# A windowed-attention kernel on one core: the order of transfers, transposes and maxima inside a slot, 32x32 masks and three-operand normalisations

## The chip, the cores and the metric

The kernel runs as one program on 1 core of one Trainium2 chip. The metric is device time in microseconds (us) from one execution, taken as the median of several runs; lower is better.

## The reference

Two layers over x of 8 batches x 1024 rows x 256 features, each with a residual: windowed attention with 16 heads of 16 features, and a linear layer with the signs of a weight.

```python
def _L0_attn_ref(x, Wq, bq, Wk, bk, Wv, bv, Wo, bo):
    ...
    q = (x @ Wq.T + bq).reshape(B, S, N_HEADS, D_K)
    k = (x @ Wk.T + bk).reshape(B, S, N_HEADS, D_K)
    v = (x @ Wv.T + bv).reshape(B, S, N_HEADS, D_K)
    scores = jnp.einsum('bqhd,bkhd->bhqk', q, k) * SCALE
    scores = jnp.where(mask, scores, jnp.float32(-10000.0))   # key j with i - 128 <= j <= i
    attn = jax.nn.softmax(scores, axis=-1) + jnp.float32(1e-09)
    ctx = jnp.einsum('bhqk,bkhd->bqhd', attn, v).reshape(B, S, D_MODEL)
    return ctx @ Wo.T + bo
x = x + _L0_attn_ref(_layernorm(x), ...)
x = x + jnp.einsum('bsi,oi->bso', _layernorm(x), jnp.sign(weight))
```

## The kernel before

The rows are cut in tiles of 128, eight to a batch (t = 0 to 7), 64 in all, and two neighbouring tiles make a pair. All engines run the same loop of 64 **slots**, one for each tile, and four more for what is left over; the function slot of each engine is an order written out by hand, and semaphores alone connect the engines. In slot t the engines work on many tiles at once (function parts): the scores and the exponentials of tile t, the row maxima of tile t+3 (mx) and their transpose for tile t+2 (nm), probabilities times values of tile t-1 (pv), the output projection of tile t-3 (op), the second layer of tile t-4 (ff), and the load of the residual rows for tile t-2 (xr). Work on pairs alternates: slots with odd t project queries and values of pair (t+5)/2 (tqv) and load x; slots with even t project keys of pair (t+4)/2 (k) and compute the statistics and the first layer normalisation (ln). Below, an odd slot and an even one are meant in this sense, and the two together are called a slot pair.

**TensorE** computes, in a slot: scores in eight steps (two heads each, into two banks sc), the transposes of the unnormalised sums u (turn_u, into bank ga), the transpose of the maxima (turn_max), three groups of masked maximum scores (max_scores, bank mx), three groups of pv, and the projections. turn_u writes ga, so it waits until VectorE has read the output projection of the tile before it out of ga (semaphore x2_done). In max_scores a matmul of the 128x128 identity with a window of zeros and -1e30 first writes the mask of 2 or 3 heads for one of two row groups; 32x32 tiles with 16 rows of contraction then add the scores, 8 at a time side by side.

**VectorE**, in the order of a slot: second normalisation (norm2, tile xn2, shown as xn<-x), reciprocal and product of the sums (normalise), row_max 0, split parts of the projections (_lo tiles), k_lo in an even slot, row_max 1, statistics (ln), the residual sums x, q_lo in an odd slot, row_max 2, first normalisation norm1 in an even slot (xn<-xs), then the sum x2 = ga + xr, which releases turn_u of the next slot, and its statistics (mv) for norm2 of the next slot.

**GpSimd (POOL)**: two affine selects on 128x1024 values (mask_probs) for the second half of the heads of tile t-1, sum_v in an even slot, add_biases (adds brow to xr, which must have landed), rsqrt1 in an even slot (rs1 for norm1), mask_probs for the first half of tile t, and rsqrt2 (rs2 for norm2).

**SyncE (SP)** issues nearly all DMAs, in order; a wait holds back everything behind it. The queries in three parts are copied from the layout of the projection to q_stack by six DMAs for a pair (stack_q), behind two for q_max; the keys likewise (stack_k, set_k_max). stack_q stands in the odd slot in which the queries are projected, and waits for q_16, the last of ScalarE's copies of them. The lines after it in that slot are the load of xr and the store of y:

```python
                if part["tqv"]:
                    stack_q(*part["tqv"])
                if part["k"]:
                    set_k_max(*part["k"])
                if part["ks"]:
                    stack_k(*part["ks"])
                if part["xr"]:
                    load_xr(*part["xr"])
```

Of the kernel before, what the change touches and what calls it, by code (L numbers as in the profile page):

```python
# [23 lines left out]
P = 128  # L24
# [22 lines left out]
def build(nc, x, wq_t, wk_t, wv_t, wo_t, wf_t, bq_c, bk_c, bv_c, bo_r, out):  # L47
# [7 lines left out]
    with ExitStack() as ctx:  # L55
# [22 lines left out]
        window = sb("window", [P, 3, WIN], BF16)  # L78
        window0 = sb("window0", [P, 3, WIN], BF16)
# [122 lines left out]
        def parts(b, t):  # L202
# [34 lines left out]
        def _(sp):  # L237
# [6 lines left out]
            def stack_q(b, p):  # L244
                i, _ = halves(p)
                cols = slice(2 * P * p, 2 * P * (p + 1))
# [4 lines left out]
                for c in range(C):  # L251
                    sp.dma_start(q_max[64 * c:64 * c + DK, :, 2 * P * (g % 2):2 * P * (g % 2 + 1)],
                                 q_16[:, c, :]).then_inc(q_max_set[i], 16)
                wait(sp, sc_filled, SC_FILLS * (TILES * (b - 1) + 2 * p + 2))
# [4 lines left out]
                for c in range(C):  # L259
                    for r, src in enumerate((q_hi, q_hi, q_lo)):  # L260
                        at = 64 * c + DK * r
                        sp.dma_start(q_stack[at:at + DK, :, cols].bitcast(F32),  # L262
                                     src[:, c, :].bitcast(F32)).then_inc(q_stacked[i], 16)
# [27 lines left out]
            def stack_nmax(b, t):  # L291
                i, _ = halves(t)
                sp.wait_ge(nm_done, TILES * b + t + 1)
                for c in range(C):
# [10 lines left out]
            def slot(b, t):  # L305
                now, part = parts(b, t)
                if part["nm"]:
                    stack_nmax(*part["nm"])
                if part["load"]:
                    load_x(*part["load"])  # L310
                if part["tqv"]:
                    stack_q(*part["tqv"])
                if part["k"]:
                    set_k_max(*part["k"])
                if part["ks"]:
                    stack_k(*part["ks"])
                if part["xr"]:
                    load_xr(*part["xr"])
# [9 lines left out]
            stack_q(0, 0)  # L328
# [8 lines left out]
            stack_q(0, 1)  # L337
# [4 lines left out]
            stack_q(0, 2)  # L342
# [5 lines left out]
        def _(pool):  # L348
# [8 lines left out]
            g.memset(window[:, 0, :], 0.0)  # L357
            g.memset(window0[:, 0, :], 0.0).then_inc(pool_setup, 1)
# [4 lines left out]
            def make_windows():  # L363


                n = 3
                for mask in (window, window0):
                    for blk in range(P // QB):
                        m = mask[QB * blk:QB * (blk + 1), 0, :]
                        for base, cm, step in ((0, -1, 1), (P, 1, -1)):  # L370
                            pool.wait_ge(pool_setup, n)
                            g.affine_select(out=m, in_=m, compare_op=ALU.is_ge, fill=MASKED, base=base,
                                            pattern=[[step, WIN]], channel_multiplier=cm).then_inc(pool_setup, 1)
                            n += 1
                for blk in range(P // QB):
                    m = window0[QB * blk:QB * (blk + 1), 0, :]
                    pool.wait_ge(pool_setup, n)
                    g.affine_select(out=m, in_=m, compare_op=ALU.is_ge, fill=MASKED, base=QB * blk - P,
                                    pattern=[[1, WIN]], channel_multiplier=0).then_inc(pool_setup, 1)
                    n += 1  # L380
                pool.wait_ge(pool_setup, n)

                for mask in (window, window0):
                    for h in (1, 2):
                        last = g.tensor_copy(mask[:, h, :], mask[:, 0, :])
                last.then_inc(windows_done, 1)
# [74 lines left out]
        def _(act):  # L461
# [79 lines left out]
            def nmax_part(b, t):  # L541
# [4 lines left out]
                wait(act, nmax_stacked[i], 32 * (TILES // 2 * b + m))  # L546
# [76 lines left out]
        def _(dve):  # L623
# [20 lines left out]
            def norm1(b, p):  # L644
# [6 lines left out]
                for j in range(2):  # L651
                    last = v.tensor_scalar(xn[:, j], xs[:, i, j], mv1[:, j, 0:1], rs1[:, j:j + 1],  # L652
                                           ALU.subtract, ALU.mult)
                last.then_inc(xn_done, 1)

            def norm2(b, t):
# [5 lines left out]
                v.tensor_scalar(xn2[:, :], x2[:, i], mv2[:, 0:1], rs2[:, :],  # L662
                                ALU.subtract, ALU.mult).then_inc(xn2_done, 1)
# [66 lines left out]
            def slot(b, t):  # L730
                now, part = parts(b, t)
                if part["ff"]:
                    norm2(*part["ff"])
                if part["op"]:
                    normalise(*part["op"])
                if part["mx"]:
                    row_max(*part["mx"], 0)
# [93 lines left out]
        def _(pe):  # L831
# [72 lines left out]
            def max_scores(b, t, i, turns=(mx_banks,)):  # L904
# [10 lines left out]
                hs = slice(0, len(heads))  # L915
                for rg in range(C):
                    dst = banks[:, rg, 0:WIN * len(heads)].rearrange("p (h e k) -> p h e k", h=len(heads), k=QB)
                    if t == 0:
# [283 lines left out]
```

## Time and profile before

| | |
|---|---|
| median of 3 runs | 953.24 us (949.41, 953.24 and 1605.7) |
| profiled execution | 948.12 us, of which the traced span is 946.4 us |
| TensorE busy | 788.6 us, 83% |
| VectorE busy | 630.9 us, 67% |
| ScalarE busy | 487.9 us, 52% |
| GpSimd busy | 443.9 us, 47% |
| mean granted TensorE clock | 0.887 |

The chain of waits starts at the last instruction and goes back to what released each. A share of it belongs to work that nothing hid. The timeline shows instructions in order, merged where equal ones follow each other; the bracket at a row's end is the idle time of that engine ahead of it and what ended it.

### The profile page before, as it was taken

To read this page: it belongs to the slowest core of one execution; us is meant where nothing else is said; L and a number is where in the kernel's file an instruction comes from. 1 tells how busy PE (TensorE), PEld (TensorE's weight loads), DVE (VectorE), ACT (ScalarE), POOL (GpSimd) and SP (SyncE) were. 2 spreads that over 40 slices of the span, in tenths; PEclk is the share of its full clock that TensorE was granted. 3 is DMA by queue.
4 is the path that set the end of the run, shared out by engine and by line. 5 is a ranking of instruction groups with operands and counts; after the bars stand their busy time and mean duration, and the time that the engine had idled before them with its cause. 6 is when DMAs were issued, how large, how long until landed. Compare 5 with 4: busy or idle time off the path is not lost.

```text
span 946.4 us, 29257 instructions
## 1 busy us (share of the span) xinstructions
PE 788.6 (83%) x11920; PEld 643.7 (68%) x11920; DVE 630.9 (67%) x1171; ACT 487.9 (52%) x1029; POOL 443.9 (47%) x596
## 2 busy tenths in 40 slices
PE   2679898888888988888988888899888899888984
PEld 2467677776677766777776766777666777766763
DVE  6555667676767766776667766667667677666543
ACT  2245665555556554555645555565545565454640
POOL 6324444545535453544445454354444444545551
PEclk9767999889889997989979998988988999887995
DMA  3884656556646555775556677555567645457310
GB/s 94 113 105 84 106 93 97 94 83 114 113 79 106 90 94 88 114 113 85 89 86 102 95 114 109 93 95 83 86 106 113 102 86 87 92 79 108 65 34 22
DMA packets 105077, 87.80 MB, mean 93 GB/s; under 512 B 12336, under 2 KB 104944, under 8 KB 104944
## 3 DMA queue, kind: packets, MB, share of 16 engines
q1 hardware_dynamic: 103008, 84.49, 55.8%
q8 instruction: 95, 1.56, 0.8%
q10 hardware_dynamic: 1936, 1.45, 0.5%
q14 instruction: 38, 0.31, 0.1%
HBM read 18.22 MB, written 8.39 MB: 28 GB/s over the span
## 4 chain that ended last, share of the span: by engine, by line
PE 49%; DMA 15%; SPq 12%; DVE 10%; issue 6%; POOL 6%; ACT 1%; POOLq 0%; DVEq 0%; ACTq 0%
DMA xr<-x 14%; SPq L262 12%; PE sc L965 10%; PE gc L838 10%; PE pv L983 8%; PE ga L838 6%; PE mx L931 4%; DVE xn L652 4%; PE ga L994 2%; POOL rs L394 2%; POOL xr L428 2%; PE gc L853 2%; PE mx L923 2%; PE gb L1023 1%; DVE x L779 1%
## 5 line engine op out<-in xcount | busy, mean ns | idle before, releaser
L537 ACT ACTIVATE prob<-sc 128x512 f32<-128x512 f32 x448 | 264.3, 596 | 216.5 <-PE sc L965 212.6
L965 PE MATMUL sc<-q_stack,k_stack 128*128 128x256 f32 (+1 forms) x1024 | 249.9, 334 | 5.2 <-DMA q_stack<-q_hi 2.5
L965 PEld LDWEIGHTS sc<-q_stack,k_stack 128*128 128x128 f32 x1024 | 171.7, 210 | 53.7 <-issue 45.7
L695 DVE TENSOR_REDUCE nmax<-mx 128x6 f32<-128x960 f32 x188 | 195.1, 1038 | 10.0 <-PE mx L931 5.6
L983 PE MATMUL pv<-prob,v_ones 128*32 128x128 f32 x3840 | 159.0, 297 | 0.0
L420 POOL TENSOR_SCALAR_AFFINE_SELECT prob<-prob 128x1024 f32<-128x1024 f32 x128 | 143.9, 1124 | 5.9 <-ACT prob L539 5.9
L428 POOL TENSOR_TENSOR xr<-xr,brow 128x256 f32<-128x256 f32 x64 | 46.7, 730 | 189.6 <-DMA xr<-x 172.7
L417 POOL TENSOR_SCALAR_AFFINE_SELECT prob<-prob 128x1024 f32<-128x1024 f32 x112 | 122.3, 1092 | 25.1 <-ACT prob L537 25.1
L994 PE MATMUL ga<-ident,u 128*128 128x128 f32 x256 | 45.6, 307 | 89.8 <-DVE x L779 89.6
L983 PEld LDWEIGHTS pv<-prob,v_ones 128*32 128x32 f32 x3840 | 100.2, 116 | 29.5 <-issue 8.6
L433 POOL TENSOR_SCALAR ve<-mv 128x1 f32<-128x1 f32 x64 | 13.9, 217 | 222.0 <-DVE mv L790 222.0
L662 DVE TENSOR_SCALAR xn<-x,mv,rs 128x256 f32<-128x256 f32 x64 | 73.0, 1141 | 63.1 <-POOL rs L435 63.1
L652 DVE TENSOR_SCALAR xn<-xs,mv,rs 128x256 f32<-128x256 f32 x64 | 68.3, 1107 | 47.9 <-POOL rs L394 47.9
L994 PEld LDWEIGHTS ga<-ident,u 128*128 128x128 f32 x256 | 32.1, 156 | 95.4 <-issue 93.1
L931 PE MATMUL mx<-k_max,q_max 16*32 16x160 bf16 x4008 | 77.8, 252 | 0.0
L923 PE MATMUL mx<-window,ident 128*128 128x192 bf16 x330 | 59.5, 267 | 19.2 <-DVE nmax L695 19.2
L675 DVE SCALAR_TENSOR_TENSOR q_lo<-gc,bq,q_hi 128x256 fp32r<-128x256 f32 x64 | 28.0, 480 | 63.0 <-ACT q_hi L488 63.0
L547 ACT ACTIVATE nmax_t<-gb 16x128 fp32r<-16x128 f32 x64 | 16.5, 258 | 102.7 <-PE gb L943 102.7
L931 PEld LDWEIGHTS mx<-k_max,q_max 16*32 16x32 bf16 x4008 | 36.2, 94 | 37.7 <-issue 32.2
L409 POOL TENSOR_TENSOR vsum<-vsum,v_ones 128x256 f32<-128x256 f32 x56 | 41.6, 743 | 21.7 <-ACT v_ones L522 19.2
L539 ACT ACTIVATE prob<-sc 128x256 f32<-128x256 f32 x64 | 24.8, 387 | 47.8 <-PE sc L965 47.6
L683 DVE SCALAR_TENSOR_TENSOR k_lo<-gc,bk,k_hi 128x256 fp32r<-128x256 f32 x60 | 26.3, 480 | 32.3 <-ACT k_hi L499 32.3
(136 smaller groups left out, 1501.8 us busy)
## 6 DMA issues: line engine op xcount, KB each, us to landing
q_stack<-q_hi SPq DMA_DIRECT2D x128, 128.0 KB, 4.6
k_stack<-k_hi SPq DMA_DIRECT2D x128, 128.0 KB
xs<-x SPq DMA_DIRECT2D x32, 256.0 KB, 3.4
q_stack<-q_lo SPq DMA_DIRECT2D x64, 128.0 KB, 4.7
k_stack<-k_lo SPq DMA_DIRECT2D x64, 128.0 KB
xr<-x SPq DMA_DIRECT2D x64, 128.0 KB, 4.9
out<-x SPq DMA_DIRECT2D x64, 128.0 KB, 4.5
q_max<-q SPq DMA_DIRECT2D x64, 64.0 KB
```

Of the source, the lines that this page charges most:

```text
L262: sp.dma_start(q_stack[at:at + DK, :, cols].bitcast(F32), src[:, c, :].bitcast(F32)).then_inc(q_stacked[i], 16)
L417: g.affine_select(out=nxt, in_=nxt, compare_op=ALU.is_ge, fill=0.0, base=0, pattern=[[0, HB], [-1, P]], channel_multiplier=1)
L420: g.affine_select(out=own, in_=own, compare_op=ALU.is_ge, fill=0.0, base=0, pattern=[[0, HB], [1, P]], channel_multiplier=-1).then_inc(pro ...
L537: a.activation(prob[:, own:nxt + 1:nxt - own, 2 * f:2 * f + 2, :], sc, ACT.Exp, scale=SCALE).then_inc(exp_done, 1)
L652: last = v.tensor_scalar(xn[:, j], xs[:, i, j], mv1[:, j, 0:1], rs1[:, j:j + 1], ALU.subtract, ALU.mult)
L695: v.tensor_reduce(nmax[:, n % 2, :].rearrange("p (r h) -> p r h", r=C)[:, :, h0:h0 + m], banks[:, :, 0:WIN * m].rearrange("p r (h k) -> p ...
L838: last = mm(dst, l, r, start=j == 0, stop=j == len(terms) - 1)
L923: mm(dst[:, :, ends, :], ident16[:, :], window[:, hs, :].rearrange("p h (e k) -> p h e k", k=QB)[:, :, ends, :], start=True, stop=False, s ...
L931: last = mm(banks[QB * blk:QB * (blk + 1), rg, WIN * j:WIN * (j + 1)], q_max[64 * rg:64 * rg + DK, h, aq:aq + QB], k_max[64 * rg:64 * rg + ...
L965: last = mm(sc_bank[f % 2][:, 2 * P * j:2 * P * j + q], k_stack[:, h, ak:ak + P], q_stack[:, h % HB, P * t:P * t + q], start=True, stop=True)
L983: last = mm(pv_bank[32 * j:32 * (j + 1), P * cg:P * (cg + 1)], v_ones[:, tile, h, :], prob[:, part, h, :], start=cg == 0 and k == 0, stop= ...
L994: last = nc.tensor.transpose(ga[:, P * cg:P * (cg + 1)], u[:, t % 2, P * cg:P * (cg + 1)], ident[:, :])
```

## The change

SP: the load of xr comes first in a slot; stack_q is split by half (c) and moved from the odd slot into the even slot after it, with k_max between its halves; stack_k moves from the even slot to the odd one behind it; the two small DMAs for the maxima of a tile become one that writes partitions 48 and 112. TensorE: turn_u stands behind the first group of maxima and of pv; the mask of a group of maxima is written by eight 32x32 matmuls (4 blocks of queries, 2 row groups) from a mask of 32 rows, broadcast over the heads, in place of two 128x128 ones. VectorE: row_max 0 stands ahead of normalise; both normalisations are scalar_tensor_tensor with the reciprocal deviation as a broadcast tensor, in place of tensor_scalar with two per-row scalars. GpSimd: ten affine selects build the masks at the start in place of twenty and four copies.

```diff
-                         "tqv": pair(5), "k": pair(4), "ks": pair(2), "ln": pair(6), "load": pair(7)}
+                         "tqv": pair(5), "k": pair(4), "ks": pair(1), "ln": pair(6), "load": pair(7)}
...
             def slot(b, t):
                 now, part = parts(b, t)
+                if part["xr"]:
+                    load_xr(*part["xr"])
+                if part["ks"]:
+                    stack_k(*part["ks"])
                 if part["nm"]:
                     stack_nmax(*part["nm"])
                 if part["load"]:
                     load_x(*part["load"])
-                if part["tqv"]:
-                    stack_q(*part["tqv"])
                 if part["k"]:
+                    set_q_max(*part["k"])
+                    stack_q(*part["k"], 0)
                     set_k_max(*part["k"])
-                if part["ks"]:
-                    stack_k(*part["ks"])
-                if part["xr"]:
-                    load_xr(*part["xr"])
+                    stack_q(*part["k"], 1)
...
             def stack_nmax(b, t):
                 i, _ = halves(t)
                 sp.wait_ge(nm_done, TILES * b + t + 1)
-                for c in range(C):
-                    at = 64 * c + 3 * DK
-                    sp.dma_start(q_stack[at:at + 1, :, P * t:P * (t + 1)].bitcast(F32),
-                                 nmax_t[HB * c:HB * (c + 1), i, :].bitcast(F32)).then_inc(nmax_stacked[i], 16)
+                at = 3 * DK
+                sp.dma_start(q_stack[at:at + 65:64, :, P * t:P * (t + 1)].bitcast(F32),
+                             nmax_t[:, i, :].bitcast(F32)).then_inc(nmax_stacked[i], 16)
...
             stack_nmax(0, 1)
-            stack_q(0, 2)
             run(sp, slot)
...
-                    last = v.tensor_scalar(xn[:, j], xs[:, i, j], mv1[:, j, 0:1], rs1[:, j:j + 1],
-                                           ALU.subtract, ALU.mult)
+                    last = v.scalar_tensor_tensor(xn[:, j], xs[:, i, j], mv1[:, j, 0:1],
+                                                  rs1[:, j:j + 1].broadcast_to([P, D]), ALU.subtract, ALU.mult)
...
-                v.tensor_scalar(xn2[:, :], x2[:, i], mv2[:, 0:1], rs2[:, :],
-                                ALU.subtract, ALU.mult).then_inc(xn2_done, 1)
+                v.scalar_tensor_tensor(xn2[:, :], x2[:, i], mv2[:, 0:1], rs2[:, :].broadcast_to([P, D]),
+                                       ALU.subtract, ALU.mult).then_inc(xn2_done, 1)
...
-                hs = slice(0, len(heads))
-                for rg in range(C):
-                    dst = banks[:, rg, 0:WIN * len(heads)].rearrange("p (h e k) -> p h e k", h=len(heads), k=QB)
...
-                        mm(dst[:, :, ends, :], ident16[:, :],
-                           window[:, hs, :].rearrange("p h (e k) -> p h e k", k=QB)[:, :, ends, :],
+                m = len(heads)
+                for blk in range(P // QB):
+                    for rg in range(C):
+                        rows = slice(64 * rg, 64 * rg + QB)
+                        dst = banks[QB * blk:QB * (blk + 1), rg, 0:WIN * m].rearrange("p (h e k) -> p h e k", h=m, k=QB)
+                        if t == 0:
+                            mask = window0[rows, blk, :].rearrange("p (e k) -> p e k", k=QB)
+                        else:
+                            mask = edges[rows, :, :]
+                            dst = dst[:, :, 0:WIN // QB:WIN // QB - 1, :]
+                        mm(dst, ident16[rows, rows], mask.unsqueeze(1).broadcast_to(list(dst.shape)),
                            start=True, stop=False, skip_group_check=True)
```

SP's queue over one odd slot and the even slot after it, before. The odd slot's part begins with the maxima and the load of xs; the even slot's with the second nmax_t row:

```order
L296 DMA q_stack<-nmax_t 1x8x128 x2
L242 DMA xs<-x 128x2x256
L252 DMA q_max<-q 16x8x256 x2
L262 DMA q_stack<-q_hi 16x8x256 x2
L262 DMA q_stack<-q_lo 16x8x256
...
L303 DMA xr<-x 128x256
L323 DMA out<-x 128x256
L296 DMA q_stack<-nmax_t 1x8x128 x2
L272 DMA k_max<-k 16x8x256 x2
L288 DMA k_stack<-k_hi 16x8x256
...
L303 DMA xr<-x 128x256
```

The same stretch of SP's queue now, odd slot first:

```order
L306 DMA xr<-x 128x256
L292 DMA k_stack<-k_hi 16x8x256
...
L299 DMA q_stack<-nmax_t 2x8x128
L242 DMA xs<-x 128x2x256
L327 DMA out<-x 128x256
L306 DMA xr<-x 128x256
L299 DMA q_stack<-nmax_t 2x8x128
L251 DMA q_max<-q 16x8x256 x2
L266 DMA q_stack<-q_hi 16x8x256 x2
L266 DMA q_stack<-q_lo 16x8x256
L276 DMA k_max<-k 16x8x256 x2
```

xr no longer stands behind a transfer of the queries, and queries and keys have changed slots.

TensorE from the end of an odd slot into the even one, before:

```order
L965 MATMUL sc<-q_stack,k_stack 128x256 x2
L994 MATMUL ga<-ident,u 128x128 x4
L943 MATMUL gb<-ident,nmax 16x128
L965 MATMUL sc<-q_stack,k_stack 128x256 x2
L923 MATMUL mx<-window,ident 128x3x2x32 x2
L931 MATMUL mx<-k_max,q_max 32x160 x24
L983 MATMUL pv<-prob,v_ones 32x128 x8
```

And now:

```order
L965 MATMUL sc<-q_stack,k_stack 128x256 x2
L943 MATMUL gb<-ident,nmax 16x128
L965 MATMUL sc<-q_stack,k_stack 128x256 x2
L924 MATMUL mx<-edges,ident 32x3x2x32 x8
L931 MATMUL mx<-k_max,q_max 32x160 x24
L983 MATMUL pv<-prob,v_ones 32x128 x8
L994 MATMUL ga<-ident,u 128x128 x4
```

The transposes of u, with their wait for x2_done, have moved behind one transpose, one step of scores, the first maxima and the first pv; the mask is eight matmuls instead of two.

VectorE at the start of an even slot, before:

```order
L662 TENSOR_SCALAR xn<-x,mv,rs 128x256
L704 RECIPROCAL rden<-ga 128x16
L708 TENSOR_TENSOR cx<-ga,rden 128x256
L695 TENSOR_REDUCE nmax<-mx 128x2x3
L744 TENSOR_TENSOR t_lo<-gb,t_hi 128x256
```

And now:

```order
L661 SCALAR_TENSOR_TENSOR xn<-x,mv,rs 128x256
L694 TENSOR_REDUCE nmax<-mx 128x2x3
L703 RECIPROCAL rden<-ga 128x16
L707 TENSOR_TENSOR cx<-ga,rden 128x256
L743 TENSOR_TENSOR t_lo<-gb,t_hi 128x256
```

The first maxima no longer stand behind the sums.

## Rows read from the trace of the kernel before

**Rows 1.** The page: busy shares, and the granted TensorE clock in 40 slices.
```profile
PE 788.6 (83%) x11920; PEld 643.7 (68%) x11920; DVE 630.9 (67%) x1171; ACT 487.9 (52%) x1029; POOL 443.9 (47%) x596
PEclk9767999889889997989979998988988999887995
```

**Rows 2.** Who waited for whom: total us, times, longest us.
```profile
POOL xr L428 <- DMA xr<-x: 172.7, 43, 7.2
PE ga L994 <- DVE x L779: 89.6, 32, 4.0
SPq L250 <- ACT q L505: 267.4, 30, 11.3
```

**Rows 3.** The chain of waits from 192 to 225 us: start, length, what.
```profile
187.87 5.13 DMA xr<-x
...
195.98 1.17 DVE xn L652
...
215.07 1.88 SPq L262
```

**Rows 4.** TensorE's timeline from 283.5 to 311 us.
```profile
287.91 0.34 PE L923 MATMUL mx<-window,ident 128*128 128x192 bf16 x2 [1.01 <-DVE nmax L695]
...
299.71 0.34 PE L923 MATMUL mx<-window,ident 128*128 128x192 bf16 x2
299.98 0.40 PE L931 MATMUL mx<-k_max,q_max 16*32 16x160 bf16 x24
300.30 0.65 PE L983 MATMUL pv<-prob,v_ones 128*32 128x128 f32 x16
...
309.29 0.83 PE L994 MATMUL ga<-ident,u 128*128 128x128 f32 x4 [2.89 <-DVE x L779]
```

**Rows 5.** Two stretches, an odd slot and an even one: busy us by engine, clock.
```profile
284.00:295.30 11.30, 10.25 (x161) 8.33 (x160) 8.13 (x16) 7.11 (x15) 5.75 (x7) 1.00 0.45 74
295.30:306.40 11.10, 10.65 (x189) 8.73 (x187) 7.46 (x15) 7.48 (x17) 5.90 (x9) 1.00 0.80 131
```

**Rows 6.** VectorE's timeline from 283.5 to 311 us.
```profile
294.15 0.41 DVE L779 TENSOR_TENSOR x<-ga,xr 128x256 f32<-128x256 f32 x1
...
296.23 1.17 DVE L662 TENSOR_SCALAR xn<-x,mv,rs 128x256 f32<-128x256 f32 x1 [0.99 <-POOL rs L435]
...
303.41 0.25 DVE L641 BATCH_NORM_AGGREGATE mv<-st 128x2 f32<-128x6 f32 x2
...
306.55 2.26 DVE L652 TENSOR_SCALAR xn<-xs,mv,rs 128x256 f32<-128x256 f32 x2 [1.52 <-POOL rs L394]
```

**Rows 7.** GpSimd's timeline of the same stretch.
```profile
304.79 0.73 POOL L428 TENSOR_TENSOR xr<-xr,brow 128x256 f32<-128x256 f32 x1 [4.93 <-DMA xr<-x]
...
305.80 0.72 POOL L394 TENSOR_TENSOR rs<-ve,half 128x2 f32<-128x2 f32 x1
306.48 1.09 POOL L417 TENSOR_SCALAR_AFFINE_SELECT prob<-prob 128x1024 f32<-128x1024 f32 x1
```

**Rows 8.** The second normalisation over the run: ns least/median/most; and what cb_lo took twice.
```profile
L662 DVE TENSOR_SCALAR xn<-x,mv,rs x64: 414/1164/1167, 103.3 to 940.4; 128x256 f32<-128x256 f32 x64
...
92.11 1.19 DVE L724 TENSOR_TENSOR cb_lo<-brow,cb_hi 128x256 fp32r<-128x256 f32 x1
198.37 0.43 DVE L724 TENSOR_TENSOR cb_lo<-brow,cb_hi 128x256 fp32r<-128x256 f32 x1
```

**Rows 9.** GpSimd's timeline beside the first of these cb_lo.
```profile
91.86 1.17 POOL L417 TENSOR_SCALAR_AFFINE_SELECT prob<-prob 128x1024 f32<-128x1024 f32 x1 [0.77 <-ACT prob L537]
92.98 1.27 POOL L420 TENSOR_SCALAR_AFFINE_SELECT prob<-prob 128x1024 f32<-128x1024 f32 x1
```

**Rows 10.** TensorE at the loop's first slot; turn_max (L943) over the run, first and last start.
```profile
55.50 0.77 PE L965 MATMUL sc<-q_stack,k_stack 128*128 128x256 f32 x2 [2.54 <-DMA q_stack<-q_hi]
56.07 0.41 PE L943 MATMUL gb<-ident,nmax 128*16 128x128 f32 x1
...
L943 PE MATMUL gb<-ident,nmax x64: 271/273/421, 41.0 to 890.2; 128*16 128x128 f32 x64
```

More of the change, by code:

```diff
@@ L253, in stack_q @@
                                  q_16[:, c, :]).then_inc(q_max_set[i], 16)
+            def stack_q(b, p, c):
+                i, _ = halves(p)
+                cols = slice(2 * P * p, 2 * P * (p + 1))
+                g = PAIRS * b + p
                 wait(sp, sc_filled, SC_FILLS * (TILES * (b - 1) + 2 * p + 2))
@@ L327, in _ @@
             load_x(0, 2)
-            stack_q(0, 0)
+            set_q_max(0, 0)
+            for c in range(C):
+                stack_q(0, 0, c)
             set_k_max(0, 0)
@@ L336, in _ @@
             load_x(0, 3)
-            stack_q(0, 1)
+            set_q_max(0, 1)
+            for c in range(C):
+                stack_q(0, 1, c)
             set_k_max(0, 1)
@@ L363, in make_windows @@
             def make_windows():
[L366 to L385, printed above, removed]
@@ L386, in make_windows @@
-                last.then_inc(windows_done, 1)
+                for rg in range(C):
+                    rows = slice(64 * rg, 64 * rg + QB)
+                    pool.wait_ge(pool_setup, 3)
+                    g.affine_select(out=edges[rows, 0, :], in_=edges[rows, 0, :], compare_op=ALU.is_ge, fill=MASKED,
+                                    base=0, pattern=[[1, QB]], channel_multiplier=-1).then_inc(windows_done, 1)
+                    g.affine_select(out=edges[rows, 1, :], in_=edges[rows, 1, :], compare_op=ALU.is_ge, fill=MASKED,
+                                    base=0, pattern=[[-1, QB]], channel_multiplier=1).then_inc(windows_done, 1)
+                    m = window0[rows, :, :]
+                    for k, (base, cm, step, per) in enumerate(((0, -1, 1, 0), (P, 1, -1, 0), (-P, 0, 1, QB))):
+                        pool.wait_ge(pool_setup, 3 + 2 * rg + k)
+                        g.affine_select(out=m, in_=m, compare_op=ALU.is_ge, fill=MASKED, base=base,
+                                        pattern=[[per, P // QB], [step, WIN]],
+                                        channel_multiplier=cm).then_inc(pool_setup if k < 2 else windows_done, 1)
@@ L733, in slot @@
                     norm2(*part["ff"])
+                if part["mx"]:
+                    row_max(*part["mx"], 0)
                 if part["op"]:
                     normalise(*part["op"])
-                if part["mx"]:
-                    row_max(*part["mx"], 0)
                 if part["tqv"]:
@@ L914, in max_scores @@
                 banks = turns[(MXG * n + i) % len(turns)]
-                hs = slice(0, len(heads))
-                for rg in range(C):
-                    dst = banks[:, rg, 0:WIN * len(heads)].rearrange("p (h e k) -> p h e k", h=len(heads), k=QB)
-                    if t == 0:
-                        mm(dst, ident16[:, :], window0[:, hs, :].rearrange("p h (e k) -> p h e k", k=QB),
-                           start=True, stop=False, skip_group_check=True)
-                    else:
-                        ends = slice(0, WIN // QB, WIN // QB - 1)
-                        mm(dst[:, :, ends, :], ident16[:, :],
-                           window[:, hs, :].rearrange("p h (e k) -> p h e k", k=QB)[:, :, ends, :],
+                m = len(heads)
+                for blk in range(P // QB):
+                    for rg in range(C):
+                        rows = slice(64 * rg, 64 * rg + QB)
+                        dst = banks[QB * blk:QB * (blk + 1), rg, 0:WIN * m].rearrange("p (h e k) -> p h e k", h=m, k=QB)
[5 more added lines that the diff above has]
+                        mm(dst, ident16[rows, rows], mask.unsqueeze(1).broadcast_to(list(dst.shape)),
                            start=True, stop=False, skip_group_check=True)
@@ L1066, in slot @@
                     scores(b, t, 0)
-                if op:
-                    turn_u(*op)
                 if part["nm"]:
@@ L1076, in slot @@
                     prob_v(*pv, 0)
+                if op:
+                    turn_u(*op)
                 if now:
```

27 lines of the change are left out of this document (13 added, 14 removed).

## The prediction

> **What bounds the kernel now.** Begin with the page: TensorE is busy 83% of the span and no other engine over 67%, yet the granted clock keeps dipping [rows 1]. So there are holes in TensorE's work. Next, who waited for whom [rows 2]: TensorE lost 89.6 us in 32 waits at the transposes of u (L994), put down to VectorE's sum x2 (L779). That is one wait of 2.8 us for each slot pair. GpSimd lost 172.7 us waiting for the transfer of xr, and SP 267.4 us for the copy q_16 (L505).
>
> The chain of waits says how these three belong together [rows 3]. It repeats with every slot pair: SP issues the six query copies (L262), then the xr transfer (5.13 us with its issue), then GpSimd adds brow to xr and, behind that in its queue, makes rs1 (L394), which lets VectorE do norm1 (L652, xn), the sum x2, and only then may TensorE transpose u and go on to the next queries, whose q_16 SP waits for. It is a closed loop through two slots.
>
> How fast is it? turn_max (L943) stands once in every slot; slot 0 has its start at 56.07 and slot 61 the last at 890.2 [rows 10]. That is 834.1 us for 61 slots, 13.67 each, 27.35 a slot pair, and 30.5 pairs. The rest, about 112 us, is start and tail.
>
> For one pair at full clock see [rows 5]: the odd slot is 11.30 us with 10.25 busy, the even one 11.10 with 10.65 busy, and behind it comes the wait of 2.89 us [rows 4]. The other holes are 1.01 us, for row_max 0 of VectorE, in the odd slot [rows 4] and some 0.45 in the even one. After the long hole the clock falls: turn_u takes 0.83 us there, and the page shows sevens to nines all along [rows 1].
>
> **The change part by part.**
>
> *xr first on SP, queries a slot later.* The load of xr no longer stands behind q_16 and has more than a slot to land. The loop is open. What is late next? Take the even slot that starts at 295.30. The statistics for norm1 were there at 303.41 + 0.25 = 303.66 [rows 6], while GpSimd waited 4.93 us for xr and had rs1 at 305.80 + 0.72 = 306.52 [rows 7]. Released by the statistics, rs1 takes some 1.1 us (two small instructions) and is there at 304.8. VectorE had been idle for 1.52 us when norm1 began at 306.55 [rows 6], so from 305.03, and is just about free. norm1 took 2.26 us beside GpSimd's selects and would end near 307.25, not at 308.81: 1.55 us earlier. The saving is half of the 2.89 us hole, not all of it.
>
> *turn_u behind the first maxima and pv.* Between the old and the new place stand turn_max, a step of scores, mask, maxima and pv. By the starts in [rows 4] (299.71 to 299.98, to 300.30, and 0.57 for a pv of 16) and with the smaller mask, that is about 1.8 us of work in the hole. TensorE, through with its even slot at about 305.2, comes to turn_u at 307.0; the x2 sum ends at 307.65. A wait of 0.65 us is left. But the sum also starts a second chain: from the start of a sum x2 to that of norm2 it is 296.23 - 294.15 = 2.1 us [rows 6] (sum, statistics, two GpSimd instructions), then norm2. I get norm2 done at 307.25 + 2.1 + 1.3 = 310.65. TensorE reaches turn_x2, which needs it, after turn_u, scores and four transposes at 309.05: **1.6 us of waiting**, new in this size. row_max 0 (1.1 us), now directly behind norm2, ends at 311.75, against 311.2 at which TensorE wants the bank for the second maxima: 0.6 more; the second layer then waits 0.3 for t_lo. Together 3.15 us of holes in the odd slot and, by the same walk, 0.5 in the even one (row_max 1 behind k_lo). Of before, that was 2.89 + 1.01 + 0.45 = 4.35.
>
> *Normalisations.* norm2 takes 1164 ns in the median and 414 at least [rows 8]. Each rs is followed by a select on GpSimd, so that a norm starts just behind it (norm1 at 306.55, the select at 306.48) [rows 6, 7]: it waits for the select and then needs little. Would three operands avoid that? The only instruction with two tensors from SBUF that meets a select is the first cb_lo: 1.19 us instead of 0.43 [rows 8]. The select beside it ran from 91.86 to 93.03 [rows 9], and cb_lo ended at 93.30, 0.27 later; a norm ends some 0.16 behind its select. So the new form should be about 0.13 us longer, not shorter: 1.3 us. Bounds: 0.43 if it passes the select freely, 2.5 if it waits for both selects. I take 1.3, the row with the same operands. The next select then was 1.27 long instead of 1.14 [rows 9], 0.13 on GpSimd, which is idle half the time. 128 instructions by 0.13 are 17 us of VectorE; the share that lies on the chain is in the walk above.
>
> The Trainium skill, SBUF — State Buffer, section Who interferes with whom, says that a VectorE instruction with two SBUF inputs contends with a GpSimd instruction that reads SBUF, and that the later one stands still until the other ends. It speaks against this part of the change, and by that rule the trace agrees with the 1.19 us of cb_lo; without it the sum would be that of the free normalisation below.
>
> *Masks.* Two matmuls of 192 columns occupied 0.27 us before the maxima began (299.71 to 299.98) [rows 4]. Maxima on 32x32 tiles go side by side: 24 in 0.32 us (299.98 to 300.30), 13 ns each. Eight with 192 columns would take 8 x 13 x 1.2 = 0.13 us. Bounds: 0.1, and 0.7 if they ran one by one at the full array's pace. I take 0.13: 0.14 saved, three times a slot, 0.9 us a pair with the switch between shapes.
>
> *Keys later, queries by halves, one nmax transfer.* No cost: keys are read a slot later still. k_max has the least room. An estimate from the same two slots: k_16 is done some 6 us into the even slot, then come 1.3 us of issue and about 2.5 of landing, against 10.7 us at which the maxima of the next slot begin. That leaves 0.9 us of cover; a longer delay would at first lie inside the wait at turn_u.
>
> *Start.* Slot 0 waited 2.54 us for a query transfer [rows 10]; six of the transfers ahead of it are gone: 2.5 us saved. The tail has six norm2 in series: +1 us.
>
> **The sum.** TensorE's work in a pair is 10.25 + 10.65 = 20.9 us, plus 1.15 because the tile of that odd slot is the second of its batch and has half the pv, less 0.9 for masks: 21.15. With 3.65 of holes 24.8, and over a batch, which has short tiles at its ends, 24.5. The clock: the new holes are shorter and scattered. The hole of 1.01 us [rows 4] left the clock at 1.00 [rows 5], that of 2.89 did not, and 1.6 lies between. I charge 0.35 us a pair, between 0 and 1.2. So 27.35 - 24.85 = 2.5 us, by 30.5 pairs = 76 us; 948.1 - 76 - 2.5 + 1 = 870.6, taken as **870**. The profiled execution is 5 us under the median shown and 1 us under the lowest run, so the number stands for both. Within this case: a clock without loss (24.5) gives 860, one at its worst (25.7) 896, and masks or waits off by 0.5 us a pair add 15 either way: **845 to 900**.
>
> **The rivals.**
> - *The normalisation passes the selects freely* (0.43 us). Then norm1 ends 1.3 us earlier, norm2 0.9, and the holes at turn_u, turn_x2 and the second maxima close: about 22.6 us a pair, 948 - 145 = **803**. For it: shorter VectorE work everywhere. Against it: the cb_lo row. By the rule of the skill it doesn't happen.
> - *The hole only moves.* The walk assumes that VectorE's instructions fit without slack lost; if the wait at turn_x2 becomes 2.5 us and the clock dips in each pair as now, a pair is some 26.1: 948 - 38 = **910**. For it: VectorE has 20 us of work in a pair of 24.5. Against it: holes before added up to 4.35 at 27.35.
> - *Slower.* The three-operand form is let through only when GpSimd is between queues, so behind both selects: 2.5 us. norm2 is then 1.2 later in each of 61 slots (73 us), norm1 1.2 in 30 pairs (36 us): 870 + 109 = **979**. It decides from 1.8 us for a norm2 upward. Against it: cb_lo slipped in ahead of the second select.
> - *The change doesn't do what it says*, xr still being late because SP is held by y or k_16 in the slot before: then only masks, start and 1.8 us of cover are left, near 915, inside the second rival.
>
> **How the numbers follow.** The forecast 0.69; free normalisation 0.12; hole moves 0.14; slower 0.05. The range, 820 to 910, reaches below the middle between forecast and first rival and up to the second; it leaves out most of the first rival, the upper half of the second and the last. 2% is about what a measurement of this kernel can tell from no change, 934 to 972 us. Faster 0.9, within 2% 0.06, slower 0.04.
>
> **What would show it.** POOL waiting for xr gone, SP's wait for L505 far smaller, the xr transfer no longer in the chain; norm2 at 1.3 us median; the largest wait of TensorE at turn_x2 (L1023) for norm2, some 1.5 us a pair; the mask's group under 0.15 us; granted clock over 0.95; turn_max every 12.4 us. I am wrong if norm2 is at 0.45, if k_max shows up as what TensorE waits for, or if the clock stays at 0.89 with fewer holes.

## The result, and the profile after

The changed kernel takes 898.02 us (896.23 to 900.61, 4 runs). Its ratio to the kernel before is 0.943, with a 95% interval of 0.936 to 0.949: faster, by 5.7%. The forecast was 870 us with a range of 820 to 910. Its profiled execution has a span of 895.2 us. Two executions lie far outside all others and count in no figure here: one of 1605.7 us of the kernel before, and one of 3429.6 us in run 6.

The page of the changed kernel: busy shares, and the granted clock in 40 slices.

```profile
PE 744.8 (83%) x13072; PEld 617.3 (69%) x13072; DVE 638.8 (71%) x1171; ACT 484.2 (54%) x1029; POOL 453.1 (51%) x582
PEclk9788999889999899999999899999999988899995
```

Against [rows 1] TensorE's share is the same 83%, of a shorter span. The mean granted clock went from 0.887 to 0.926: there are more nines, and still sevens and eights.

Who waited for whom, in the changed kernel: total us, times, longest us; the last row is SP's own.

```profile
PE gb L1023 <- DVE xn L661: 58.3, 36, 2.7
PE mx L924 <- DVE nmax L694: 30.0, 53, 2.1
PE ga L994 <- DVE x L778: 2.1, 6, 0.6
POOL xr L427 <- DVE brow L727: 21.1, 8, 3.6
POOL ve L391 <- DVE mv L640: 111.6, 32, 8.1
SPq L306 <- DVE x L778: 176.2, 61, 7.1
```

This answers to [rows 2]. GpSimd's 172.7 us of waiting for the transfer of xr are gone; it now waits for the statistics of VectorE (L640) before rs1. TensorE's 89.6 us at turn_u (L994) have become 2.1 us, and 58.3 us are now spent at turn_x2 (L1023), which needs norm2 (L661); in the kernel before it was 11.3 us. SP waits for x2 before the load of xr, with nobody in want of it, and its waits for q_16, 267.4 us before, are down to 12.2.

TensorE's timeline from 285 to 312 us, over slots t = 2 and t = 3 of a batch.

```profile
290.68 0.50 PE L965 MATMUL sc<-q_stack,k_stack 128*128 128x256 f32 x2 [0.34 <-ACT prob L536]
291.12 0.28 PE L924 MATMUL mx<-edges,ident 32*32 32x192 bf16 x8
291.21 0.39 PE L931 MATMUL mx<-k_max,q_max 16*32 16x160 bf16 x24
...
292.11 0.66 PE L994 MATMUL ga<-ident,u 128*128 128x128 f32 x4
292.52 0.49 PE L965 MATMUL sc<-q_stack,k_stack 128*128 128x256 f32 x2
292.84 0.60 PE L852 MATMUL gc<-ident,xn 128*128 128x128 f32 x4
295.85 0.44 PE L1023 MATMUL gb<-ident,xn 128*128 128x128 f32 x2 [2.40 <-DVE xn L661]
296.04 0.48 PE L965 MATMUL sc<-q_stack,k_stack 128*128 128x256 f32 x2
297.63 0.47 PE L837 MATMUL ga<-wh_o,cb_hi 128*128 128x256 f32 x2 [1.11 <-DVE cx L707]
...
302.13 0.63 PE L837 MATMUL gc<-xt_hi,wh_q 128*128 128x256 f32 x2
```

turn_u goes without a wait. Then comes the new hole, here 2.40 us, and 1.11 more for cx in front of the bias projection. The last row shows the price that follows: a step of the projection takes 0.63 us where it takes 0.40 at full clock. The mask occupies 0.09 us (291.12 to 291.21) where it was 0.27 [rows 4].

VectorE's timeline of the same stretch shows the chain that ends in that hole.

```profile
288.93 2.39 DVE L651 SCALAR_TENSOR_TENSOR xn<-xs,mv,rs 128x256 f32<-128x256 f32 x2
291.24 0.41 DVE L778 TENSOR_TENSOR x<-ga,xr 128x256 f32<-128x256 f32 x1
291.58 0.59 DVE L716 TENSOR_SCALAR brow<-gc,bvs 128x128 f32<-128x128 f32 x2
292.21 0.29 DVE L721 CAST cb_hi<-brow 128x256 fp32r<-128x256 f32 x1
292.54 0.43 DVE L723 TENSOR_TENSOR cb_lo<-brow,cb_hi 128x256 fp32r<-128x256 f32 x1
292.88 0.42 DVE L785 BATCH_NORM_STATS2 st<-x 128x6 f32<-128x256 f32 x1
...
294.50 1.30 DVE L661 SCALAR_TENSOR_TENSOR xn<-x,mv,rs 128x256 f32<-128x256 f32 x1 [0.98 <-POOL rs L434]
```

norm1 takes 2.39 us (2.26 in [rows 6]), norm2 1.30, and in this slot spread_bias (L716 to L723) stands between x2 and its statistics for another 1.3 us.

norm2 over the run, as in [rows 8], and turn_max, as in [rows 10]: least, median, most, first and last start.

```profile
L661 DVE SCALAR_TENSOR_TENSOR xn<-x,mv,rs x64: 485/1296/1298, 100.2 to 889.1; 128x256 f32<-128x256 f32 x64
...
L943 PE MATMUL gb<-ident,nmax x64: 269/272/380, 42.2 to 837.5; 128*16 128x128 f32 x64
```

Slot 0 has its turn_max at 54.2, the last one starts at 837.5: 783.3 us for 61 slots, where it was 834.1. The start gave 1.9 us and the tail cost 1.5.

The four slots t = 0 to 3 of the third batch, bounded by turn_max: length, busy us of PE, PEld, DVE, ACT and POOL, clock, DMA share, GB/s.

```profile
255.63:265.62 9.99, 9.45 (x202) 7.94 (x199) 8.27 (x16) 7.07 (x16) 5.63 (x8) 1.00 0.52 98
265.62:279.68 14.06, 11.17 (x186) 8.96 (x183) 10.77 (x20) 8.36 (x19) 7.41 (x10) 1.00 0.81 119
279.68:290.07 10.39, 9.85 (x205) 8.37 (x203) 8.65 (x17) 7.12 (x16) 7.23 (x10) 1.00 0.62 96
290.07:309.53 19.46, 15.61 (x224) 13.03 (x221) 12.25 (x25) 8.27 (x18) 7.28 (x10) 0.82 0.56 89
```

The first two are a pair at full clock, 24.05 us. The next two take 29.85: the odd slot alone 5.4 us longer, with the clock at 0.82.

The 61 slots together, first in the changed kernel and then in run 12 below, which has the same instructions on TensorE in the same order and a clock that hardly falls:

```profile
54.21:837.49 783.28, 680.31 (x12282) 564.60 (x12280) 578.76 (x1061) 450.47 (x959) 407.18 (x516) 0.94 0.62 102
```
```profile
54.40:731.79 677.39, 639.33 (x12280) 536.96 (x12279) 485.10 (x1061) 447.60 (x959) 393.19 (x516) 0.99 0.74 118
```

TensorE is idle for 103.0 us of the changed kernel's slots, 3.4 us a pair, and busy for 41 us more than in run 12 with the same work.

### The profile page after: what moved, and what is told of

It is laid out like the page before. It is cut to its first block, busy times and chain, and to the rows that moved or that the text cites. A ratio compares the mean times of both kernels' runs of the same rounds, so it can differ in the third digit from the quotient of the medians.

```text
span 895.2 us, 31506 instructions
## 1 busy us (share of the span) xinstructions
PE 744.8 (83%) x13072; PEld 617.3 (69%) x13072; DVE 638.8 (71%) x1171; ACT 484.2 (54%) x1029; POOL 453.1 (51%) x582
## 4 chain that ended last, share of the span: by engine, by line
PE 48%; DVE 32%; issue 11%; POOL 3%; ACT 2%; SPq 2%; DMA 1%; DVEq 0%; POOLq 0%; ACTq 0%
PE gc L837 16%; DVE nmax L694 9%; PE sc L965 9%; PE pv L983 8%; PE ga L837 7%; DVE xn L651 6%; PE mx L924 2%; POOL rs L434 2%; DVE st L635 2%; PE mx L931 2%; PE ga L994 2%; PE gb L1006 2%; DVE st L785 2%; DVE k_lo L682 2%; ACT k_hi L498 2%
## 5 line engine op out<-in xcount | busy, mean ns | idle before, releaser
L965 PE MATMUL sc<-q_stack,k_stack 128*128 128x256 f32 (+1 forms) x1024 | 229.4, 316 | 14.0 <-ACT prob L536 11.0
L965 PEld LDWEIGHTS sc<-q_stack,k_stack 128*128 128x128 f32 x1024 | 159.0, 197 | 52.4 <-issue 30.3
L419 POOL TENSOR_SCALAR_AFFINE_SELECT prob<-prob 128x1024 f32<-128x1024 f32 x128 | 154.9, 1210 | 0.0
L661 DVE SCALAR_TENSOR_TENSOR xn<-x,mv,rs 128x256 f32<-128x256 f32 x64 | 81.4, 1272 | 63.4 <-POOL rs L434 63.4
L416 POOL TENSOR_SCALAR_AFFINE_SELECT prob<-prob 128x1024 f32<-128x1024 f32 x112 | 122.8, 1096 | 7.5 <-ACT prob L536 7.5
L1023 PE MATMUL gb<-ident,xn 128*128 128x128 f32 x128 | 27.4, 297 | 58.3 <-DVE xn L661 58.3
L651 DVE SCALAR_TENSOR_TENSOR xn<-xs,mv,rs 128x256 f32<-128x256 f32 x64 | 72.3, 1168 | 3.2 <-POOL rs L393 3.2
L924 PE MATMUL mx<-edges,ident 32*32 32x192 bf16 (+1 forms) x1320 | 44.8, 248 | 26.8 <-DVE nmax L694 25.2
L565 ACT ACTIVATE t_hi<-gb 128x256 fp32r<-128x256 f32 x64 | 24.6, 384 | 73.4 <-PE gb L1023 73.2
L1023 PEld LDWEIGHTS gb<-ident,xn 128*128 128x128 f32 x128 | 14.1, 143 | 66.8 <-DVE xn L661 66.8
L924 PEld LDWEIGHTS mx<-edges,ident 32*32 32x32 bf16 x1320 | 18.6, 88 | 52.2 <-DVE nmax L694 34.5
```

The source lines that it names most:

```text
L416: g.affine_select(out=nxt, in_=nxt, compare_op=ALU.is_ge, fill=0.0, base=0, pattern=[[0, HB], [-1, P]], channel_multiplier=1)
L419: g.affine_select(out=own, in_=own, compare_op=ALU.is_ge, fill=0.0, base=0, pattern=[[0, HB], [1, P]], channel_multiplier=-1).then_inc(pro ...
L651: last = v.scalar_tensor_tensor(xn[:, j], xs[:, i, j], mv1[:, j, 0:1], rs1[:, j:j + 1].broadcast_to([P, D]), ALU.subtract, ALU.mult)
L661: v.scalar_tensor_tensor(xn2[:, :], x2[:, i], mv2[:, 0:1], rs2[:, :].broadcast_to([P, D]), ALU.subtract, ALU.mult).then_inc(xn2_done, 1)
L924: mm(dst, ident16[rows, rows], mask.unsqueeze(1).broadcast_to(list(dst.shape)), start=True, stop=False, skip_group_check=True)
L965: last = mm(sc_bank[f % 2][:, 2 * P * j:2 * P * j + q], k_stack[:, h, ak:ak + P], q_stack[:, h % HB, P * t:P * t + q], start=True, stop=True)
```

## The experiments

All ratios are to the kernel before, run beside it on the same chip. The runs come from three chips, so small differences between them are better read from the ratios.

**1. SP's order alone, on the kernel before.** The edit, whose load_xr stands first in a slot:

```diff
+                if part["xr"]:
+                    load_xr(*part["xr"])
+                if part["ks"]:
+                    stack_k(*part["ks"])
...
-                if part["tqv"]:
-                    stack_q(*part["tqv"])
...
+                    set_q_max(*part["k"])
+                    stack_q(*part["k"], 0)
                     set_k_max(*part["k"])
...
+                    stack_q(*part["k"], 1)
```

> The kernel before with SP's new order alone (xr first, keys in the odd slot, queries by halves in the even one). If the closed loop through q_16, SP and xr is what held the kernel, the sum x2 of even slots comes 1.5 us earlier, TensorE still waits some 1.4 us at turn_u, and the clock dips less: 2 us a slot pair by 30.5 pairs and 2.5 us at the start, so 948 - 64 = about 885, between 875 and 905; GpSimd's wait for xr is gone. Rival, that the place of turn_u brings the gain: 935 to 950.

Measured: 868.0 us, ratio 0.912 (0.906 to 0.918). This one part is faster than the whole change. Its waits:

```profile
PE ga L1002 <- DVE x L787: 41.7, 31, 1.7
```

The wait at turn_u (here L1002) is 41.7 us in 31, down from 89.6. GpSimd no longer waits for xr. The mean clock is 0.958.

**2. turn_u moved alone, with row_max 0 ahead of normalise, on the kernel before.** VectorE's part of the edit stands last.

```diff
                     scores(b, t, 0)
-                if op:
-                    turn_u(*op)
...
                     prob_v(*pv, 0)
+                if op:
+                    turn_u(*op)
...
+                if part["mx"]:
+                    row_max(*part["mx"], 0)
                 if part["op"]:
                     normalise(*part["op"])
-                if part["mx"]:
-                    row_max(*part["mx"], 0)
```

> The kernel before with turn_u behind the first maxima and pv and row_max 0 ahead of normalise, nothing else. By the loop theory xr still waits for q_16, but turn_u no longer holds up the way to the next queries: 0.7 to 1.5 us a pair, 948 - 34 = about 915, between 900 and 930, with GpSimd's wait for xr as before and the wait of TensorE now at turn_x2. Rival, that only SP's order matters: 940 to 950.

Measured: 959.15 us, ratio 1.008 (1.004 to 1.012): a little slower, and neither expectation. The rival came nearer. Its waits:

```profile
PE gb L1023 <- DVE xn L662: 49.4, 34, 2.6
...
POOL xr L428 <- DMA xr<-x: 177.5, 43, 7.0
...
PE pv L983 <- POOL prob L420: 28.7, 24, 2.3
```

The loop is as closed as before (177.5 us for xr). What I had left out: GpSimd's selects of the first half of the heads stand behind xr in its queue too, and pv, now ahead of turn_u, waits 28.7 us for them.

**3. The old normalisations, on the changed kernel.**

```diff
-                    last = v.scalar_tensor_tensor(xn[:, j], xs[:, i, j], mv1[:, j, 0:1],
-                                                  rs1[:, j:j + 1].broadcast_to([P, D]), ALU.subtract, ALU.mult)
+                    last = v.tensor_scalar(xn[:, j], xs[:, i, j], mv1[:, j, 0:1], rs1[:, j:j + 1],
+                                           ALU.subtract, ALU.mult)
```

> The changed kernel with both normalisations as tensor_scalar again. By the select theory norm2 goes from 1272 to about 1165 ns and norm1 from 2.39 to 2.26 us a pair; both stand in the chain that ends in TensorE's wait at turn_x2, 0.25 us a pair: 898 - 8 = 890, between 882 and 896. Rival, that the three-operand form is a gain: 903 or more.

Measured: 876.39 us, ratio 0.921 (0.916 to 0.927). The direction is that of the collision theory, the size nearly three times my 8 us. norm2 is at 1141 ns in the mean instead of 1272, and the mean clock at 0.936 instead of 0.926. TensorE has 10 us less of idle time (140.7 us of the span, where it was 150.4) and is busy for 11 us less with the same work (733.7, 744.8).

**4. The old masks, on the changed kernel** (two 128x128 matmuls for a group instead of eight 32x32; the way GpSimd builds them at the start goes back too).

```diff
-                for blk in range(P // QB):
-                    for rg in range(C):
...
-                        mm(dst, ident16[rows, rows], mask.unsqueeze(1).broadcast_to(list(dst.shape)),
...
+                for rg in range(C):
...
+                        mm(dst[:, :, ends, :], ident16[:, :],
+                           window[:, hs, :].rearrange("p h (e k) -> p h e k", k=QB)[:, :, ends, :],
```

> The changed kernel with the masks as two 128x128 matmuls again. A mask costs 0.10 us more of TensorE, six times a pair; the one ahead of the hole at turn_x2 and the ones in front of a wait for row_max are covered, so 0.3 us a pair: 898 + 9 = 907, between 900 and 913. Rival, that the masks bring nothing because VectorE's chain sets the pace: 898.

Measured: 901.61 us, ratio 0.947 (0.939 to 0.954), against 0.943 (0.936 to 0.949) of the changed kernel. The intervals overlap: the masks are worth some 4 us or nothing. The pages tell where their gain went. TensorE is busy for 761.0 us with the old masks and for 744.8 with the new, 16 us less, but idle for 139.1 us of the span with the old and for 150.4 with the new.

**5. Only xr first, on the kernel before.** One edit, load_xr from the end of SP's slot to its head.

```diff
+                if part["xr"]:
+                    load_xr(*part["xr"])
                 if part["nm"]:
                     stack_nmax(*part["nm"])
...
-                if part["xr"]:
-                    load_xr(*part["xr"])
```

> The kernel before with one edit: the load of xr stands first in SP's slot, everything else in its old place (queries still behind q_16 in the odd slot). If it is only xr behind q_16 that closes the loop, this gives nearly all of the 84 us of the new SP order: 875, between 862 and 890. Rival, that the shift of queries and keys to other slots, with more even DMA load, is needed too: 905 or more.

Measured: 869.54 us, ratio 0.917 (0.914 to 0.920). Two moved lines give as much as the whole new order. A slot pair of this kernel, bounded by turn_max:

```profile
250.06:262.10 12.04, 10.06 (x184) 8.15 (x182) 10.36 (x20) 7.70 (x17) 6.26 (x8) 1.00 0.84 141
262.10:274.13 12.03, 10.98 (x168) 9.04 (x166) 8.18 (x16) 7.69 (x16) 6.29 (x9) 1.00 0.47 83
```

24.07 us, the same as the pair of the changed kernel, with a wait of 1.54 us at turn_u. But here such pairs are the rule: over the 61 slots the clock is 0.98, and 0.94 in the changed kernel.

**6. GpSimd's selects ahead of rsqrt1, on the changed kernel.**

```diff
+                if now:
+                    mask_probs(*now, 0)
                 if part["ln"]:
                     rsqrt1(*part["ln"])
-                if now:
-                    mask_probs(*now, 0)
```

> The changed kernel with GpSimd's two selects for tile t ahead of rsqrt1, so that norm1 meets no select. By the collision theory norm1 falls from 2.39 to about 0.9 us a pair, x2 and norm2 of the next slot come 1.5 us earlier, and the hole at turn_x2 shrinks: 1.5 us a pair and some clock, 898 - 55 = 843, between 830 and 860. Rival, that norm1's length is its own and not the select's: 895 to 900.

Measured: 835.07 us, ratio 0.879 (0.875 to 0.883). norm1 over the run, with the row of the changed kernel behind it:

```profile
L651 DVE SCALAR_TENSOR_TENSOR xn<-xs,mv,rs x64: 469/476/1316, 13.8 to 726.6; 128x256 f32<-128x256 f32 x64
```
```profile
L651 DVE SCALAR_TENSOR_TENSOR xn<-xs,mv,rs x64: 475/1174/1308, 13.8 to 790.6; 128x256 f32<-128x256 f32 x64
```

The same instruction takes 476 ns instead of 1174 when no select runs beside it. Its length was the select's, as expected, and 63 us went with it: the waits at turn_x2 fell from 58.3 us to 19.7.

**7. turn_u and normalise back in their old places, on the changed kernel** (the edit of run 2 reversed).

> The changed kernel with turn_u and normalise in their old places, three-operand normalisations kept. From the two runs that have one of them each (868 with the SP order alone, 876 with the turned order, masks and the old normalisations), late transposes cost: normalise and bias_proj stand behind a norm2 that comes late, in slot t = 3 above all. Then 880, between 870 and 890. The prediction's step, that the move fills a hole with 1.8 us of work, would give 920 or more.

Measured: 904.33 us, ratio 0.955 (0.950 to 0.960). My 880 was wrong; the changed kernel is better, by 6 us in the medians and by 0.012 in the ratio (0.943, 0.936 to 0.949), with intervals that all but touch. A pair of this kernel, and the wait ahead of its second slot:

```profile
333.88:346.07 12.19, 9.64 (x202) 8.02 (x200) 10.73 (x20) 7.44 (x17) 7.55 (x9) 1.00 0.52 99
346.07:358.57 12.50, 12.50 (x218) 10.88 (x215) 8.49 (x17) 6.29 (x16) 5.67 (x9) 0.86 0.56 119
```
```profile
345.60 0.63 PE L994 MATMUL ga<-ident,u 128*128 128x128 f32 x4 [2.01 <-DVE x L778]
```

The wait is 2.01 us, half a microsecond longer than in run 5, and the next slot has the clock at 0.86 and no idle time. The mean clock is 0.889. The three-operand form seems to cost more with turn_u early (904 against 868 of run 1, which also lacks the new masks and the single transfer of the maxima) than with it late (898 against 876 of run 3); the first pair differs in more than the form, so this is not shown.

**8. No normalisation meets a select.** The kernel of run 7, with tensor_scalar, the edit of run 6, spread_bias behind the statistics, and one wait on GpSimd:

```diff
                 now, part = parts(b, t)
+                if part["ff"]:
+                    pool.wait_ge(xn2_done, TILES * part["ff"][0] + part["ff"][1] + 1)
                 if part["pv"]:
                     mask_probs(*part["pv"], 1)
```

> The changed kernel with the old places of turn_u and normalise, tensor_scalar normalisations, the selects of tile t ahead of rsqrt1, the selects of tile t-1 waiting for norm2, and spread_bias behind the statistics of x2. No normalisation meets a select: norm1 0.8 us a pair and norm2 0.41 each. TensorE then is nearly without holes: some 21.8 us a pair, 115 + 30.5 x 21.8 = 780, between 770 and 815. If another wait takes over (ScalarE's exponentials, k_max), 830 or more.

Measured: 785.81 us, ratio 0.828 (0.825 to 0.831), the best of both kernels and all runs. norm2 over the run, and a pair:

```profile
L663 DVE TENSOR_SCALAR xn<-x,mv,rs x64: 407/412/415, 99.6 to 778.0; 128x256 f32<-128x256 f32 x64
```
```profile
233.97:244.50 10.53, 9.71 (x201) 8.03 (x199) 8.28 (x20) 7.54 (x17) 6.30 (x8) 1.00 0.52 89
244.50:255.59 11.09, 10.49 (x186) 9.00 (x183) 7.43 (x16) 7.81 (x17) 6.29 (x9) 1.00 1.01 153
```

norm2 takes 412 ns in every slot. 21.6 us a pair is close to TensorE's own work; the mean clock is 0.969. The select that waits for norm2 starts 0.52 us later, on an engine with time to spare.

**9. The three-operand form alone, on the kernel before** (the edit of run 3 reversed).

> The kernel before with one edit: both normalisations in the three-operand form. By the collision theory norm2 takes 1270 ns and norm1 2.39 us a pair, both on the closed loop, and longer waits at turn_u cost clock too: slower, 948 + 10 = 958, between 952 and 975. Rival, that the form is a gain where the loop is closed: 940 or less.

Measured: 963.63 us, ratio 1.012 (1.006 to 1.018): slower by about 1%, as expected. norm2 is at 1271 ns in the mean, TensorE's wait at turn_u at 96.8 us instead of 89.6.

**10. spread_bias behind the statistics, on the changed kernel.**

```diff
                     v.tensor_tensor(x2[:, i], ga[:, 0:D], xr[:, i], ALU.add).then_inc(x2_done, 1)
-                if now and t == 2:
-                    spread_bias(b)
...
                     v.bn_aggr(mv2[:, :], st2[:, :]).then_inc(mv2_done, 1)
+                if now and t == 2:
+                    spread_bias(b)
```

> The changed kernel with spread_bias of slot t = 2 behind the statistics of x2 instead of ahead of them. If its 1.3 us on VectorE are what makes slot t = 3 take 17.9 us (14.5 at t = 1), that slot falls to some 15.5 in each of 8 batches: 898 - 18 = 880, between 872 and 890. Rival, that bias_proj's wait for cx is what costs: 892 or more.

Measured: 894.34 us, ratio 0.938 (0.932 to 0.943), not to be told from the changed kernel. Its timeline at t = 3:

```profile
293.01 0.44 PE L1023 MATMUL gb<-ident,xn 128*128 128x128 f32 x2 [1.29 <-DVE xn L661]
294.79 0.47 PE L837 MATMUL ga<-wh_o,cb_hi 128*128 128x256 f32 x2 [1.11 <-DVE cx L707]
```

The hole at turn_x2 shrank from 2.40 to 1.29 us, as meant, and the one for cx stayed. By the starts of turn_max, the slots t = 3 fell from 17.5 to 15.8 us in the mean, as expected, but the slots t = 1 rose from 14.4 to 15.5. The mean clock did not rise (0.924) and TensorE is busy for 744.4 us as before: the dips went to other slots, and only 5 us of idle time are gone. The expectation failed on size: the other three pairs of a batch have holes of 1.5 to 1.6 us at turn_x2 of their own, and removing one of several like holes gave back little.

**11. The three-operand form in the kernel of run 8.**

> The kernel of 786 us (no normalisation meets a select) with the three-operand form in both normalisations. Without a collision the form costs only its own length, 0.49 instead of 0.42 us, three times a pair: 786 + 4 = 790, between 785 and 798. Rival, that the form itself and not the select made the changed kernel slow: 805 or more.

Measured: 789.36 us, ratio 0.828 (0.824 to 0.833), the same as run 8; norm2 takes 484 ns in the mean. Away from the selects the form costs nothing that the measurement can tell.

**12. turn_u late in the kernel of run 8** (the edit of run 2).

> The kernel of 786 us with turn_u behind the first maxima and pv, as in the changed kernel. The waits at turn_u, 0.3 us in three pairs of four, are filled; nothing else should be late, since norm2 is early and spread_bias is out of the way: 783, between 776 and 790. If normalise behind row_max 0 delays the bias projection or turn_c, 792 or more.

Measured: 788.14 us, ratio 0.827 (0.823 to 0.830), the same as run 8. With short normalisations the place of turn_u makes no difference that can be measured.

## Why the prediction was right, and where its size was off

*The loop through q_16, SP and xr: right, and alone enough.* Runs 1 and 5 show it: 868 and 870 us with nothing but SP's order, or nothing but xr ahead of the queries. The rest of the change together is a loss of 30 us against run 1.

*What is late next: right.* The wait was forecast at turn_x2 with 1.6 us in a pair and stands there with 58.3 us in 36 waits, 1.62 each. In three of the four pairs of a batch it is 1.50 to 1.61 us, as here at t = 1, and 2.40 at t = 3:

```profile
270.60 0.44 PE L1023 MATMUL gb<-ident,xn 128*128 128x128 f32 x2 [1.56 <-DVE xn L661]
```

The 0.65 us that the walk left at turn_u are nearly absent (2.1 us in all). A pair at full clock is 24.05 us, forecast 24.8.

*The three-operand form: right in kind, too small in the sum.* The prediction took 1.3 us from one cb_lo, and the median is 1296 ns. The rule of the Trainium skill (SBUF — State Buffer, Who interferes with whom) held in kind: runs 6 and 11 take the select away and the same instruction is 476 to 484 ns. Two inputs are not all that matters here, for tensor_scalar, with one tensor, is lengthened by the select too (1164 ns [rows 8], and 412 in run 8). But I let the new form count by its 0.13 us; run 3 shows it to be worth 22 us, half in idle time and half in TensorE's busy time at a lower clock. The free-normalisation rival named a prize that exists, for the wrong reason: the form doesn't pass the select, another order of GpSimd keeps the two apart.

*turn_u behind the first maxima: over-credited.* The step said that it fills a hole with 1.8 us of work. It fills that hole, and the chain x2, norm2, turn_x2 opens one of 1.6 us, which the walk had too. Alone it loses 0.8% (run 2), in the changed kernel it is worth some 6 us (run 7), in run 12 nothing.

*The term that was mis-sized, the clock.* The step was "I charge 0.35 us a pair", between 0 and 1.2, with a mean clock over 0.95; it is 0.926. Four pairs of a batch should have had 4 x 24.85 = 99.4 us. Over 61 slots the changed kernel has 783.3 / 61 x 8 = 102.7, so 3.3 us a batch too much, 25 us in the run, nearly the whole miss of 28.

The two rows of the 61 slots split it. The walk had 3.65 us of holes in a pair, and TensorE is idle for 103.0 / 30.5 = 3.4: the holes were right, a little too long. But it is busy for 680.3 us where run 12, with the same work and the clock at 0.99, has 639.3. That is 41 us, 1.3 a pair and more than the upper bound of the step, where 11 us were charged. So the clock cost some 30 us more than the sum had, and shorter holes gave 8 of them back, which leaves 22 of the 25. The number came out inside its range in part because these two errors point opposite ways. It also came out nearer to the second rival, that the hole only moves (910), than to the forecast (870); what that rival had right is the price of the clock in the main, for a wait near its 2.5 us stands in only one pair of four.

Where the clock pays is only in part known. The slot t = 3 is the longest, 17.5 us in the mean of a batch; the sum had only "short tiles" at the ends of a batch and no bias, while spread_bias lengthens the chain by 1.3 us there and cx adds 1.11. Run 10 took the 1.3 us away and won only 4 us, within the interval. Why the waits at turn_x2 went with more low clock than those of nearly the same length at turn_u in run 5 stays open.

*Masks, keys later, start.* The mask alone measured 0.09 us against 0.13 forecast, but the step ahead of it holds TensorE for 0.08 us longer (0.32 from start to start at 283.46, where it was 0.24 at 299.47). So a mask saves 0.10 us, 0.6 in a pair; 0.9 was in the sum. Run 4 agrees: 16 us of busy time, 0.5 a pair. Of these only some 5 us reached the span; the other 11 came back as idle time. The later keys cost nothing that shows: TensorE's waits for k_stack are 2.0 us in all, and there are none for k_max. The start gave 1.9 us (forecast 2.5), the tail cost 1.5 (forecast 1).

## What to carry to other kernels

Follow the chain of waits until it closes on itself, and look there for the cheapest link: here a load that nobody delayed on purpose stood behind a wait in a queue, and two lines gave 8%. When an instruction always lasts as long as what runs beside it, change when the other one runs, not the form of the instruction. And take a change apart: of the parts that went in together here, one gave nearly everything (84 us in run 1), and another took a quarter of it back (22 us in run 3). A clock that falls is seen best as TensorE's busy time for the same work, beside its idle time.

## What the runs showed of the hardware

VectorE's tensor_scalar and scalar_tensor_tensor on 128x256 float32 in SBUF take 0.41 and 0.48 us by themselves (runs 8 and 11) and 1.17 and 1.30 beside a GpSimd select of 1.09 us that started 0.07 or 0.08 us earlier. They end 0.16 and 0.28 us behind it, less than they take alone, so by the trace a part of them ran beside the select. The select behind is 1.14 us long after tensor_scalar and 1.28 after the three-operand form, and 1.09 where no normalisation meets it (run 8).

In run 5 TensorE's wait at turn_u was at most 1.67 us in a pair, in most pairs 1.16 to 1.66, and the clock over the 61 slots was 0.98 of its higher level (2.4 GHz). In run 7 it was 1.94 to 2.01 us in three pairs of four and 1.57 in the fourth, and the clock was 0.90; two slots behind such waits had it at 0.87 and 0.86. The two kernels are 35 us apart, the longer waits, the three-operand form, the masks and SP's order included, so what of this is due to the length of the wait alone is not shown.
